# Attention probabilities split into fp16 halves before the transpose, and transposed by DMA instead of TensorE

## What is computed

```python
q = rms_norm((x @ wq).reshape(B, L, 16, 128), q_norm_w)      # and rotary
k = rms_norm((x @ wk).reshape(B, L, 4, 128), k_norm_w)       # and rotary
k_ctx = rms_norm((h_ctx_kv @ wk_ctx).reshape(B, T, 4, 128), k_norm_w)
k_full = jnp.concatenate([k_ctx, k], axis=1)
v_full = jnp.concatenate([v_ctx, v], axis=1)
scores = jnp.einsum('blhd,bmhd->bhlm', q, k_full) * scale + mask
probs = jax.nn.softmax(scores, axis=-1)
out = jnp.einsum('bhlm,bmhd->blhd', probs, v_full)
out = out.reshape(B, L, NUM_HEADS * HEAD_DIM)
return out @ wo
```

## Time and profile before

| | |
|---|---|
| median of 3 runs | 377.71 us (375.49 to 378.03) |
| the profiled execution | 377.97 us |
| its span | 376.3 us |
| mean granted clock of TensorE | 0.977 of full speed |

### The profile page before, as it was taken

The page is one execution under the profiler, slowest core; times in us unless marked ns, Lnnn a source line. Parts: engine busy times, 40 slices in busy tenths (PEclk is TensorE's granted clock), DMA queues, the critical chain, the costliest instruction groups (busy, mean ns, idle before and its releaser), DMA issues.

```text
span 376.3 us, 7781 instructions
## 1 busy us (share of the span) xinstructions
PE 343.7 (91%) x2471; PEld 237.3 (63%) x2476; DVE 325.6 (87%) x625; ACT 271.2 (72%) x913; POOL 165.8 (44%) x242
## 2 busy tenths in 40 slices
PE   6697798799999999999999999999999999998994
PEld 5373555376567665866685577567666778674572
DVE  1668999998999899899989998999899897759653
ACT  3557879676986797699759876986797567167562
POOL 3356565652754275427344443644174300334330
PEclk9788989999999999999999999999999999989999
DMA  5967000000030003000000000000000000000011
GB/s 179 379 212 223 17 0 2 1 2 14 3 111 0 14 0 111 14 1 0 0 14 0 0 0 14 0 0 0 0 0 1 2 0 2 2 0 3 22 35 57
DMA packets 11603, 13.49 MB, mean 36 GB/s; under 512 B 824, under 2 KB 9024, under 8 KB 11584
## 3 DMA queue, kind: packets, MB, share of 16 engines
q1 hardware_dynamic: 11584, 13.25, 11.0%
HBM read 12.20 MB, written 1.05 MB: 35 GB/s over the span
## 4 chain that ended last, share of the span: by engine, by line
PE 40%; DVE 24%; ACT 17%; issue 10%; POOL 4%; DMA 2%; SPq 1%; DVEq 1%; ACTq 0%; POOLq 0%
PE proj L1324 10%; ACT probs L524 8%; PE pt_ps L1300 5%; DVE probs L953 5%; PE proj L1157 4%; PE turn L1246 3%; DVE nmax L941 3%; DVE pT_lo L879 3%; PE o_ps L1310 3%; POOL q_rot L744 3%; PE sc_ps L1267 2%; ACT pT_hi L435 2%; DMA wq<-in_L_xattn_wq_dram 2%; ACT q_junk L468 2%; DVE q_t L870 2%
## 5 line engine op out<-in xcount | busy, mean ns | idle before, releaser
L524 ACT ACTIVATE probs<-sc_ps,nbias,q_r 128x256 f32<-128x256 f32 x128 | 70.8, 574 | 2.8 <-DVE nbias L945 2.8
L744 POOL TENSOR_TENSOR q_rot<-q_t 128x512 f32<-128x512 f32 x32 | 41.4, 1295 | 42.8 <-DVE q_t L872 42.0
L953 DVE TENSOR_SCALAR probs<-probs,rden 128x256 f32<-128x256 f32 x128 | 51.2, 461 | 1.1
L1157 PE MATMUL proj<-wq_hi,xT 128*128 128x512 f16 x128 | 40.1, 396 | 2.9 <-DVE wq_lo L863 2.9
L435 ACT ACTIVATE pT_hi<-pt_ps 128x512 f16<-128x512 f32 x64 | 34.8, 597 | 10.9 <-PE pt_ps L1300 10.9
L468 ACT ACTIVATE q_junk<-proj 128x128 bf16<-128x128 f32 x128 | 34.0, 295 | 11.7 <-DVE q_t L872 11.7
L879 DVE SCALAR_TENSOR_TENSOR pT_lo<-pt_ps,pT_hi 128x512 f16<-128x512 f32 x64 | 41.0, 682 | 0.6 <-ACT pT_hi L435 0.6
L941 DVE TENSOR_REDUCE nmax<-sc_ps 128x4 f32<-128x1024 f32 x32 | 38.9, 1214 | 1.5 <-PE sc_ps L1289 1.5
L831 POOL TENSOR_TENSOR wq<-xn_all,weight 128x512 bf16<-128x512 f32 x16 | 17.1, 1074 | 44.1 <-DVE weight L1098 23.4
L1324 PE MATMUL proj<-wo_hi,oT_hi 128*128 128x256 f16 x128 | 34.9, 273 | 0.0
L1324 PE MATMUL proj<-wo_lo,oT_hi 128*128 128x256 f16 x128 | 34.9, 273 | 0.0
(11 more groups left out here) (216 smaller groups left out, 920.7 us busy)
## 6 DMA issues: line engine op xcount, KB each, us to landing
wq<-in_L_xattn_wq_dram SPq DMA_DIRECT2D x4, 512.0 KB, 9.1
w<-in_L_ffn_w_dram SPq DMA_DIRECT2D x2, 1024.0 KB, 10.5
wq<-in_L_xattn_wo_dram SPq DMA_DIRECT2D x1, 2048.0 KB, 8.2
ctx_b<-in_ctx_dram SPq DMA_DIRECT2D x8, 128.0 KB, 2.1
out_dram<-x_all SPq DMA_DIRECT2D x4, 256.0 KB, 2.2
x_all<-in_x_dram SPq DMA_DIRECT2D x1, 896.0 KB, 12.3
wkc<-in_L_xattn_wk_ctx_dram SPq DMA_DIRECT2D x1, 512.0 KB, 4.2
wk<-in_L_xattn_wk_dram SPq DMA_DIRECT2D x1, 512.0 KB, 5.1
```

What stands on the lines that cost most here:

```text
L524: last = nc.scalar.activation(probs[:, h, :], sc_ps[:, h, :], ACT.Exp, bias=nbias[:, h:h + 1], scale=q_r[:, g, h:h + 1], accum_out=den[:, ...
L744: nc.gpsimd.tensor_tensor(q_rot[:], q_t1[:], q_t2[:], ALU.add).then_inc(q_added, 1)
L953: last = nc.vector.tensor_scalar(probs[:, h, :], probs[:, h, :], rden[:, h:h + 1], None, ALU.mult)
L1157: last = nc.tensor.matmul(bank[:], xT[:, a, c, :], w[:, c, cols], start=(n == 0), stop=(n == 3 * DC - 1))
```

## The change

The probabilities are no longer divided in place. DVE computes the reciprocal of the sums and multiplies it with P_SCALE (`inv_den`). ACT makes the high half `p_hi` from `probs` with this scale, head by head in two pairs, still in the layout of the scores (`p_split`), and DVE the low half `p_lo` (`p_rest`). SP then issues four transposing DMAs of 128x512 fp16 for each unit (`turn_probs`), from `p_hi` and `p_lo` to `pT_hi` and `pT_lo`, which now have two slots; `p_hi` and `p_lo` have one, so that ACT and DVE wait for the DMAs of the unit before, pair by pair. PE loses `turn_probs`, and `mix` runs in two column halves, one for each pair of heads, 12 matmuls of 256 columns; in unit 0 it moves behind the projection of v. ACT and DVE lose `p_copy` and `p_low`. In ACT's list the split stands behind `q_squares` (in unit 3 ahead of it, behind the keys' copies, which now follow all four exponentials), and ahead of `kc_squares`, `in_copies`, `v_copy` and `o_copy`. `exps` waits for the low halves of the unit before. The sum of k's parts moves from DVE to POOL, ahead of `k_roots`. `wo`, w3 and w2 are loaded in quarters between the transposing DMAs. To make room, `xn2T` lies in the buffer of the experts' weights, and the router's `ahead` and `tied` in `probs`.

```diff
-        pT_hi = sb("pT_hi", [P, 2, GW], FP16)
-        pT_lo = sb("pT_lo", [P, 2, GW], FP16)
+        p_hi = sb("p_hi", [P, R, 2 * P], FP16)
+        p_lo = sb("p_lo", [P, R, 2 * P], FP16)
+        pT_hi = sb("pT_hi", [P, 2, R, 2, P], FP16)
+        pT_lo = sb("pT_lo", [P, 2, R, 2, P], FP16)
...
+            def turn_probs(b, g):
+                u = G * b + g
+                slot = u % 2
+                if u >= 2:
+                    sp.wait_ge(pv_done, u - 1)
+                for pair in range(2):
+                    heads = slice(2 * pair, 2 * pair + 2)
+                    for src, dst, split in ((p_hi, pT_hi, p_high), (p_lo, pT_lo, p_low)):
+                        sp.wait_ge(split, 2 * u + 1 + pair)
+                        sp.dma_start_transpose(dst[:, slot, heads, :, :].rearrange("p h a t -> p (h a) t"),
+                                               src[:, heads, :].rearrange("p h k -> p (h k)")).then_inc(
+                                                   d_pT[slot][pair], 16)
+
+            sp.wait_ge(w_lo, G + 1)
+            load_wo(0)
+            load_wo(1)
+            for b in range(B):
+                for g in range(G):
+                    turn_probs(b, g)
+                    if (b, g) == (0, 0):
+                        load_wo(2)
+                        load_wo(3)
+                    if g == 1 and b + 2 < B:
+                        next_ctx(b + 2)
+                    for load, r in ((load_w3, 1), (load_w2, 2)):
+                        if (b, g) in ((r, 1), (r, 2)):
+                            load(g - 1)
+                        if (b, g) == (r + 1, 0):
+                            load(2)
+                            load(3)
...
+            def p_split(b, g):
+                act.wait_ge(s_rden, G * b + g + 1)
+                for pair in range(2):
+                    if g or not (isinstance(b, int) and b == 0):
+                        landed, count = pT_landed(b, g - 1) if g else pT_landed(b - 1, G - 1)
+                        act.wait_ge(landed[pair], count)
+                    for h in (2 * pair, 2 * pair + 1):
+                        last = copy(p_hi[:, h, :], probs[:, h, :], rden[:, h:h + 1])
+                    last.then_inc(p_high, 1)
...
-                    if g or not first:
-                        p_copy(u - 1)
-                    exps(b, g, (kc_copy, k_copy) if g == 3 and not last else ())
+                    exps(b, g)
                     if g == 1 and not first and not last:
                         ln_high(b + 1)
+                    if g == 3 and not last:
+                        kc_copy(b + 1)
+                        k_copy(b + 1)
+                        p_split(b, g)
+                    if ahead_of(b, g, 2, last):
+                        q_squares(*ahead_of(b, g, 2, last))
+                    if g != 3 or last:
+                        p_split(b, g)
                     if g == 2 and not last:
                         kc_squares(b + 1)
-                    if ahead_of(b, g, 2, last):
-                        q_squares(*ahead_of(b, g, 2, last))
...
                     if g == 2 and not last:
+                        k_add(b + 1)
                         k_roots(b + 1)
                         k_scale(b + 1)
...
+            def inv_den(b, g):
                 u = G * b + g
                 dve.wait_ge(s_exp, u + 1)
-                nc.vector.reciprocal(rden[:], den[:]).then_inc(s_rden, 1)
+                nc.vector.reciprocal(inv[:], den[:]).then_inc(s_inv, 1)
+                dve.wait_ge(s_inv, u + 1)
+                nc.vector.tensor_scalar(rden[:], inv[:], P_SCALE, None, ALU.mult).then_inc(s_rden, 1)
+
+            def p_rest(b, g, pair):
+                u = G * b + g
+                dve.wait_ge(p_high, 2 * u + 1 + pair)
                 dve.wait_ge(s_rden, u + 1)
...
+                for h in (2 * pair, 2 * pair + 1):
+                    last = low(p_lo[:, h, :], probs[:, h, :], rden[:, h:h + 1], p_hi[:, h, :])
+                last.then_inc(p_low, 1)
...
                     if ahead_of(b, g, 2, last):
                         q_turn(*ahead_of(b, g, 2, last))
+                    inv_den(b, g)
+                    p_rest(b, g, 0)
                     if g == 0 and not last:
                         ln_stats(b + 1)
                         dve.wait_ge(ln_stat, b + 2)
...
                     if g == 3 and not last:
                         kc_low(b + 1)
                         k_low(b + 1)
-                    normalise(b, g)
+                    p_rest(b, g, 1)
...
-            def mix(u, g):
-
+            def mix(b, g):
+
+                u = G * b + g
                 seen(pe, o_ready, u)
-                for a in range(2):
-                    pe.wait_ge(p_ready, 2 * u + 1 + a)
-                    for i, (v, p) in enumerate(((v_hi, pT_hi), (v_lo, pT_hi), (v_hi, pT_lo))):
-                        last = nc.tensor.matmul(o_ps[:], v[:, a, g * P:(g + 1) * P], p[:, a, :],
-                                                start=(a == 0 and i == 0), stop=(a == 1 and i == 2))
+                landed, count = pT_landed(b, g)
+                for pair in range(2):
+                    pe.wait_ge(landed[pair], count)
+                    heads = slice(2 * pair, 2 * pair + 2)
+                    for a in range(2):
+                        for i, (v, p) in enumerate(((v_hi, pT_hi), (v_lo, pT_hi), (v_hi, pT_lo))):
+                            last = nc.tensor.matmul(o_ps[:, 2 * pair * P:2 * (pair + 1) * P],
+                                                    v[:, a, g * P:(g + 1) * P], p[:, g % 2, heads, a, :],
+                                                    start=(pair == 0 and a == 0 and i == 0),
+                                                    stop=(pair == 1 and a == 1 and i == 2), skip_group_check=True)
                 last.then_inc(pv_done, 1)
```

More of the change, by code:

```diff
@@ L216, in xattn_moe_kernel @@
         d_wvc = sem("d_wvc")
-        d_wo = sem("d_wo")
+        d_wo = [sem(f"d_wo{i}") for i in range(4)]
         d_tab = sem("d_tab")
@@ L220, in xattn_moe_kernel @@
         d_w1 = sem("d_w1")
-        d_w3 = sem("d_w3")
-        d_w2 = sem("d_w2")
+        d_w3 = [sem(f"d_w3_{i}") for i in range(4)]
+        d_w2 = [sem(f"d_w2_{i}") for i in range(4)]
+        d_pT = [[sem(f"d_pT{slot}_{pair}") for pair in range(2)] for slot in range(2)]
         d_sh = sem("d_sh")
@@ L755, in _ @@
             kc_roots(0)
+            k_add(0)
             k_roots(0)
@@ L1020, in row @@
                         ln_scale(b + 1)
-                    if g or not first:
-                        p_low(u - 1)
                     if g == 2 and not first:
@@ L1059, in row @@
                         o_low(u - 1, (g - 1) % G)
-                    if g == 2 and not last:
-                        k_add(b + 1)
                     if g == 0:
@@ L1396, in row @@
                         q_turn(*ahead_of(b, g, 1, last), last)
-                    if g or not first:
-                        turn_probs(b, g)
                     if first and g < 2:
@@ L1410, in row @@
                         vc(b)
-                        if not first:
-                            mix(u - 1, G - 1)
-                        else:
+                        if first:
                             pe.wait_ge(w_lo, G + 2)
                         v(b)
+                        if not first:
+                            mix(b - 1, G - 1)
                     if g == 1:
```

101 lines of the change are left out of this document (40 added, 61 removed).

## The result

The changed kernel takes 425.02 us (median of 4 runs, 423.4 to 427.24) beside 376.6 us for the kernel before on the same chip: ratio 1.129, 95% interval 1.121 to 1.136. The forecast was 398 us. It had the sign; of 48 us it had 20. The profiled spans differ by 49.0 us, and that is what has to be found.

The account below looks back on a forecast made before the run. PE (91% busy) and DVE (87%) were nearly full, but order decides: serial chains lengthen each row by 2.7 us, seven rows give 18.9, plus 1 for the tail, on 377.97: 398 us. Own case 386 to 416; range 374 to 432.

Parts of the forecast that it names:

- rival (a): Whole kernel: gaps absorb the order and rows follow PE, losing up to 28 us, 350 us at best; below 374, chance 0.12.
- rival (b): Whole kernel: no change, as the layout overprices; row 35.6 to 35.8 us, time 380 us; 376 to 386, chance 0.12.
- (c): SP's queue decides: transposes run one after another, 435 us at 2.7 us each; more than 416 us, chance 0.16.
- The key's sum: Sum of k's parts, 1.18 us a row on DVE, 1.27 on POOL: cost nothing, up to 1.2 us without cover.
- the stand before the first low half: In each unit DVE idles before its first low half until ACT has made p_hi, 1.5 to 1.9 us.
- The prices of the new instructions: Each 128x256 piece: ACT copy 0.42 us (0.285 to 0.545), DVE low half 0.36 us (0.285 to 0.55).
- 7 x 2.7 = 18.9, and 1 for the tail: Whole kernel: seven rows each 2.7 us longer (38.2 for 35.52), plus 1 us after the last exponentials.
- the last unit's own path (317.4): Tail: sums, split, low halves and landing put the last mix's second half at 317.4 us; 1 us added.
- The steps of units 1 and 2: In each row: unit 1 falls from 11.13 to 10.05 us, unit 2 rises from 8.71 to 9.85 us.
- Unit 0's sum: Unit 0 of a row: chain from exponentials to maximum and bias, 9.33 us, before 8.61.
- Unit 3's: Unit 3 of a row: exponentials, key copies, first pair, low halves and maximum sum to 9.0 us, before 7.07.
- the quiet price for p_lo: DVE's low halves of p priced as if POOL were quiet, since they come some 2 us later than q's sum.

Follow-up runs that it names:

- e6: Changed kernel with the sum of k's parts moved back from POOL to DVE, behind o's low half in unit 2; 424.37 us, ratio 1.126.
- e7: Changed kernel; POOL scales wo after wvc's low half; in the last row DVE's copies precede the reciprocal and PE turns w2 before the last mix; 424.06 us.
- e2: Changed kernel with two transposing DMAs a unit in place of four, the mix multiplying the high half in place of the low; 428.88 us, ratio 1.137.
- e10: e9 plus unread PE matmuls: 16 behind each slot's scores in row 0, 24 before the last mix but one, 12 before the router's logits; 398.27 us.
- e12: e11 without transposing p's low halves in the last two units, their mix multiplying the high half instead; 396.62 us, ratio 1.052.
- e3: Changed kernel, p's halves made later: behind v's in unit 0, kc's squares and k's turn in unit 2, k's low halves in unit 3; 410.31 us.
- e9: Changed kernel with e3's order on ACT and DVE, e7's ends, q_rot added first on POOL in unit 2, and key's sum on DVE; 403.28 us.
- e11: e10 with the last mix put back ahead of the turns of w2; 396.31 us, ratio 1.051.
- e1: Changed kernel with 34 unread small matmuls on PE behind the scores in units 1 and 3 of rows 0 to 6; 417.73 us, ratio 1.108.

## Why the prediction was wrong

Right in kind: the sign and its reason (order, not work), rival (a), that PE sets the pace, and rival (b) fall, and so does (c) in the rows. The landing was sized right (2.4 us for 2.6), an issue was not (1.26 us for 0.6), without harm in the rows. The key's sum was rightly cost at nothing in this order (e6), and the stand before the first low half is there (1.2 to 1.8 us in the row shown). The prices of the new instructions held: one p_hi follows another every 0.40 us where 0.42 was taken, a p_lo every 0.40 for 0.36, together 0.2 us a row. PE's busy time fell by 9 us and not by 25, since many of its instructions ran at half clock; at full clock (row 6) a row lost 3.0 of the 3.5 us. One row was misread: 10.5 us is not the slowest landing of the kernel before, whose page has 12.3 us for x_all; only the far end of rival (c) used it.

The step that failed is the sum, "Seven rows have all four steps of the loop: 7 x 2.7 = 18.9, and 1 for the tail". It assumed a steady full clock, rows that are all alike, and a tail of one chain. In place of it the runs show, in order of size:

- **The ends, 14.3 us missed.** Row 0 cost 7.1 us for 2.7, since the new order lets POOL begin its scaling just ahead of wvc_lo (e7 gives 3.1 back). Row 7, for which I had no term, cost 3.8, of which 1.7 by the clock, and the tail 7.1 for 1. I had laid out the last unit's own path (317.4) and not what now stands behind it on DVE and ACT: xn2T's copy waits for the low halves, the logits for that copy, the last mix for the logits. That these waits are there is shown; that they are the cause is not. With the copies moved ahead (e7) the tail is 73.2 us, with half the transposes (e2) 73.9, and with PE filled (e10 to e12) 71.7 to 72.1, so at most some 2 of the 7.1 us were won back, and the cause of the rest stays open.
- **The order in rows 1 to 6, 8.3 us missed** (24.5 for 6 x 2.7). At full clock (rows 3 and 6) the units are 9.95, 10.19, 9.98 and 9.50 against 9.33, 10.05, 9.85 and 9.0. The steps of units 1 and 2 were sized to 0.14 us. Unit 0's sum lacked rden's wait for POOL (0.64 us where it takes 0.17), the wait for ln's statistics (0.22) and twice 0.08 in the low halves, a little more than the 0.6 it was short. Unit 3's lacked the time for which ACT stands for PE's turns of keys ahead of its two copies, which are late since PE waited for q_rot.
- **The clock in rows 1 to 6, 7.6 us missed,** a term that the prediction did not have. Its source was in the trace of before: a wait of 2.56 us in row 0, with the grant at 0.5 behind it. The prediction foresaw gaps in PE and gave them no price; some of them are paid for again afterwards, at half speed.

These three, less the 1.1 us of the earlier start, make 29.1 us, and 49.0 less the forecast's 19.9 is the same.

The choice of the quiet price for p_lo was right for the changed kernel (none over 0.50 us) and right for the reason given: q's sum is over by then. It held by the order alone; in e3 the same instructions doubled.

What stays open: why the same stand in unit 1 or 3 is followed by a fall in some rows (1, 2, 4, 5) and not in others (3, 6), in which all that the profile shows of the units is alike; what holds the tail; and what of the last 1.5 us a row between e9's 36.99 and 35.52 could still be had. Splitting the transposes over the queues of two engines wasn't tried: the Trainium skill (Advanced Engine Details and Errata, X-Bar Transpose (TRN2)) says that two streams of transposes in flight at once corrupt each other's data, and no run here shows it. No version of the change came out faster than the kernel before; the nearest, e11, is 5.1% slower.

## What to carry to other kernels

Taking 28 us of transposes from the engine that is 91% busy made the kernel 48 us slower. About half of that came in the rows, because the replacement put a serial piece (a copy on one engine, a remainder on the other) right behind the exponentials, ahead of steps for which others wait; a better order of the same work gave 2.6 of 4.2 us a row back. When a step is inserted into engines that run in order, place it behind everything that another engine is about to need, and do that for the first row, the last row and the tail too, not only for the loop. And before a big elementwise instruction is put on GpSimd, see what VectorE reads from SBUF at that time: which of the two starts a tenth of a microsecond sooner can be worth 3 us.

## What the runs showed of the hardware that was not expected

- VectorE and GpSimd held each other up on instructions that read SBUF alone, whichever came second: wvc_lo 4.62 us for 1.21, divisions 5.50 for 1.14, four low halves 3.69 for 1.68, a product of 4 columns 0.83 for 0.17. What read PSUM was free: in the kernel before, cT_lo, oT_lo and the maximum ran inside POOL's scaling of wo (46.50 to 50.76) at their usual lengths:

```profile
47.23 0.41 DVE L879 SCALAR_TENSOR_TENSOR cT_lo<-turn,cT_hi 128x256 f16<-128x256 f32 x1
47.56 0.68 DVE L879 SCALAR_TENSOR_TENSOR oT_lo<-o_ps,oT_hi 128x512 f16<-128x512 f32 x1
48.16 1.21 DVE L941 TENSOR_REDUCE nmax<-sc_ps 128x4 f32<-128x1024 f32 x1
49.40 1.38 DVE L945 TENSOR_TENSOR nbias<-nmax,q_r 128x4 f32<-128x4 f32 x1
```

The last one reads SBUF alone, takes 0.16 elsewhere, and ends as POOL does.
- A transposing DMA of 128 x 512 halves keeps SP's queue for 1.26 us (1.19 the first), three times a plain issue, and lands in 2.4 us, as quick as the plain one of equal bytes (2.3). The Trainium skill (VectorE: DVE Perf Modes, The three transpose paths) gives 1309 ns for one 128x128 block; an estimate from it for four blocks in turn is 5.2 us, and the trace has 2.4. The Trainium skill (Advanced Engine Details and Errata, X-Bar Transpose (TRN2)) calls such DMAs as fast as regular ones; the trace agrees for the landing, and the section says nothing of the issue. Two lines of SP's timeline, each from issue to free:

```profile
204.32 1.19 SPq L441 DMA_TRANSPOSE pT_hi<-p_hi  x1
205.56 1.26 SPq L441 DMA_TRANSPOSE pT_lo<-p_lo  x1
```

- Behind a stand of PE of 2.2 to 2.7 us the granted clock often goes from 1.00 to 0.50 (2.4 to 1.2 GHz) for some 3.4 us; in rows 2 to 6 of e10, e11 and e12 it did so once each behind a stand of 1.44 us. In row 0 it fell during the stand of 6.7 us and was low for about as long. Matmuls that nobody reads, put into the gap, kept it at 1.00 in rows 2 to 6 (e1).
